# First stage of an attention and expert block on one core: order of projections, masks and small vector work changed

## What is computed

```python
def bi_wkv(r, k, v, w, u, time_emb):          # condition; r = x, k = v = side input
    tf = sigmoid(sum(time_emb, -1))            # one number per batch
    decay = exp(-exp(w)) * (0.5 + 0.5 * tf)    # per channel and batch
    ek, ekv = exp(min(k, 30)), exp(min(k, 30)) * v
    nf, df = forward scans of a * decay + (ekv, ek);  nb, db = the same backward
    euk = exp(min(u + k, 30))
    base = sigmoid(r) * (nf + nb - ekv + euk * v) / max(df + db - ek + euk, 1e-8)
    return base * (0.8 + 0.2 * tf)

def attn(h, Wq, Wk, Wv, Wg, Wd, Wo):           # 16 heads of 128, 4 key heads
    q, k, v = h @ Wq, h @ Wk, h @ Wv
    bias = sigmoid(q @ Wg) * (v @ Wd)          # per key position and key head
    logits = q k / sqrt(128) + bias, causal, and only where bias > 0
    return softmax(logits) v @ Wo

x = x + attn(bi_wkv(x, side, side, w, u, cond), ...)
x = x + experts(bi_wkv(x, side, side, w2, u2, cond), ...)   # 64 experts, top 8
```

## Time and profile before

| | us |
|---|---|
| three timed runs | 525.01, 524.29, 521.43 (median 524.29) |
| the profiled execution | 525.55 |
| its span, first to last instruction | 523.8 |
| mean granted TensorE clock, share of full speed | 0.957 |

### The profile page before, as it was taken

One profiled execution on the slowest core, in us unless ns is written; L12 is line 12 of the kernel. 1 busy time (PEld: TensorE's weight loads), 2 busy tenths in 40 slices (PEclk: granted clock), 3 DMA queues, 4 the chain that ended last, 5 costly groups with the idle time before them and its releaser, 6 DMA issues.

```text
span 523.8 us, 10365 instructions
## 1 busy us (share of the span) xinstructions
PE 454.5 (87%) x3069; PEld 343.3 (66%) x3069; DVE 346.8 (66%) x1206; ACT 308.9 (59%) x852; POOL 213.3 (41%) x224
## 2 busy tenths in 40 slices
PE   3487889999999889998998957869999999999474
PEld 1266677787787668786886653446777777877221
DVE  4948769559658678739859973825567777774044
ACT  4366677689586787968798670113436656665200
POOL 0323402005012265110357877403666666666700
PEclk9879899999999999999999977979999999999969
DMA  7931494100030012300029998499845555560297
GB/s 258 416 147 42 84 193 111 22 1 1 0 81 2 25 69 72 72 11 2 21 76 378 405 405 295 119 304 309 287 138 154 164 156 158 159 166 12 52 404 299
DMA packets 47318, 79.49 MB, mean 152 GB/s; under 512 B 8266, under 2 KB 31127, under 8 KB 46880
## 3 DMA queue, kind: packets, MB, share of 16 engines
q1 hardware_dynamic: 36544, 55.08, 33.7%
q0 software_dynamic: 7680, 16.93, 8.9%
q10 hardware_dynamic: 3040, 6.82, 3.9%
HBM read 56.54 MB, written 26.44 MB: 158 GB/s over the span
## 4 chain that ended last, share of the span: by engine, by line
PE 51%; DVE 16%; ACT 14%; DMA 8%; issue 5%; POOL 3%; SPq 2%; DVEq 0%; POOLq 0%; ACTq 0%
PE ps L1701 11%; PE ps L1403 8%; PE ps L1722 7%; PE ps L1528 6%; ACT lg L696 4%; DVE lg L1039 3%; ACT lg L639 3%; DMA pairs<-pair_rows 3%; PE ps L1451 2%; PE ps L1399 2%; PE ps L1401 2%; PE ps L1400 2%; POOL slot_rows L618 2%; DMA xrow<-slot_rows 2%; SPq L432 2%
## 5 line engine op out<-in xcount | busy, mean ns | idle before, releaser
L625 POOL DMA_INDIRECT pair_rows<-eout,dest x93 | 92.0, 989 | 61.6 <-ACT eout L639 39.7
L696 ACT ACTIVATE lg<-lg,mneg 128x128 f32<-128x128 f32 (+1 forms) x128 | 56.4, 442 | 26.1 <-DVE mneg L1039 26.0
L1701 PE MATMUL ps<-wts,xg 128*64 (+1 forms) x512 | 70.6, 341 | 1.1 <-DVE xg L1316 1.1
L546 POOL DMA_INDIRECT slot_rows<-rows,pair_slot x48 | 48.8, 1017 | 34.7 <-issue 23.6
L1701 PEld LDWEIGHTS ps<-wts,xg 128*64 128x64 f32 x512 | 52.5, 142 | 13.3 <-issue 5.5
L1528 PE MATMUL ps<-oT,wo_sb 128*128 128x256 f32 x240 | 54.4, 380 | 0.0
L1316 DVE COPY xg<-ps 128x512 f32<-128x512 f32 (+1 forms) x50 | 33.3, 666 | 29.7 <-PE ps L1403 26.1
L1528 PEld LDWEIGHTS ps<-oT,wo_sb 128*128 128x128 f32 x240 | 44.6, 190 | 6.2 <-ACT oT L639 0.7
L838 ACT ACTIVATE sact<-ps 128x192 f32<-128x192 f32 (+1 forms) x50 | 16.2, 324 | 52.0 <-PE ps L1701 50.0
L1722 PE MATMUL ps<-wts,aT 96*64 96x256 f32 (+1 forms) x256 | 46.0, 379 | 0.4 <-ACT aT L639 0.4
L639 ACT ACTIVATE lg<-lg,rinv 128x128 f32<-128x128 f32 (+1 forms) x128 | 45.9, 448 | 0.8 <-DVE rinv L1047 0.8
(11 more groups left out here) (237 smaller groups left out, 1189.6 us busy)
## 6 DMA issues: line engine op xcount, KB each, us to landing
wts<-in_experts_dram SPq DMA_DIRECT2D x22, 640.0 KB, 13.9
xrow<-slot_rows SPq DMA_DIRECT2D x188, 65.0 KB
pairs<-pair_rows SPq DMA_DIRECT2D x16, 512.0 KB, 9.5
wts<-in_experts_dram ACTq DMA_DIRECT2D x10, 640.0 KB, 7.0
slot_rows<-zero SPq DMA_DIRECT2D x1, 4160.0 KB, 24.0
wT<-in_wq_t_dram SPq DMA_DIRECT2D x4, 512.0 KB, 6.9
wq_raw<-in_wq_l_dram SPq DMA_DIRECT2D x1, 2048.0 KB, 14.4
wo_sb<-in_wo_l_dram SPq DMA_DIRECT2D x1, 2048.0 KB, 20.2
```

The lines of the kernel that those rows point to most:

```text
L546: nc.gpsimd.indirect_dma_start(out=slot_d, out_offset=bass.IndirectOffsetOnAxis(ap=pair_slot[:, t, k:k + 1], axis=0), in_=r[:, k, :], in_o ...
L625: nc.gpsimd.indirect_dma_start(out=pair_d, out_offset=bass.IndirectOffsetOnAxis(ap=dest[:, d:d + 1], axis=0), in_=out_rows(d), in_offset=N ...
L696: ins = nc.scalar.activation(t, t, ACT.Exp, bias=mneg[:, u % 2, c:c + 1], scale=-1.0, accum_out=rsum[:, u % 2, c:c + 1])
L1701: ins = nc.tensor.matmul(ps[h * R:(h + 1) * R, 2 + u % 2, k * I2:(k + 1) * I2], xg[u % len(xg)][:, k, cc, h * R:(h + 1) * R], moving, star ...
```

## The change

SP issues `cond_b` first instead of third. The condition's sigmoid becomes 1/(1+exp(-s)): DVE negates and caps the sum, ACT takes an exponential after the two for the decay, DVE adds one and takes the reciprocal. ACT loads the exponential's table again with a one-column instruction ahead of `hh`. The first quarter of `wql` moves from POOL to DVE, behind the gate's low part; POOL's second quarter waits for the low part of K(0,1) instead of the bias, and `masks(0)` stands ahead of the products for batch 1. The projections' order becomes G, K(0,0), B, K(0,1), Q(0,0), Q(0,1), V0, scores of round 0, Q(1,0), Q(1,1), V1, scores of round 1. The pieces of batch 1's condition are placed anew on DVE, and `join_scans` now stands behind the logits of round 1.

```diff
-        first_projs = [G, K(0,0), K(0,1), B, Q(0,0), Q(0,1), V0, V1, Q(1,0), Q(1,1)]
+        first_projs = [G, K(0,0), B, K(0,1), Q(0,0), Q(0,1), V0, Q(1,0), Q(1,1), V1]
+        AHEAD_OF_SCORES = 7                       # was 8, on PE
 SP
+            sp.dma_start(cond_b[:], ...)          # first
             sp.dma_start(by_batch(vT, 0), side_t[:, 0])
             sp.dma_start(wu[:], wu_t)
-            sp.dma_start(cond_b[:], ...)
 POOL
-            wq_low(0)
-            pool.wait_ge(bias_ready, 1)
+            pool.wait_ge(proj_lo, order[("K", 0, 1)] + 1)
             wq_low(1)
+            masks(0)
             cond_products((0, 1))
-            masks(0)
             wq_low(2)
 ACT
-            act.wait_ge(tf_sum, 1)
-            nc.scalar.activation(tf[:], tfsum[:], ACT.Sigmoid).then_inc(tf_ready, 1)
             act.wait_ge(ld_wu, 16)
             link(nc.scalar.activation(edec[:], wcols, ACT.Exp))
             nc.scalar.activation(edec[:], edec[:], ACT.Exp, scale=-1.0).then_inc(dec_ready, 1)
+            act.wait_ge(tf_sum, 1)
+            nc.scalar.activation(tf[:], tfsum[:], ACT.Exp).then_inc(tf_ready, 1)
...
+            nc.scalar.activation(scrap[:, 0:1], edec[:, 0, 0:1], ACT.Exp)
+            h_hi_part(0)
             wq_high(0)
-            h_hi_part(0)
-            G, wq_high(1), K(0,0), wq_high(2), K(0,1), B, wq_high(3), cond_exps((0, 1)), Q(0,0), Q(0,1), V0, V1
+            G, wq_high(1), K(0,0), B, cond_exps((0, 1)), K(0,1), Q(0,0), wq_high(2), Q(0,1), wq_high(3), V0
             softmax_exp(0)
             Q(1,0), Q(1,1)
             normalise(0)
+            V1
 DVE
+            V.tensor_scalar(tfsum[:], tfsum[:], -1.0, SIG_CAP, ALU.mult, ALU.min).then_inc(tf_sum, 1)
...
+            link(V.tensor_scalar(tf[:], tf[:], 1.0, None, ALU.add))
+            link(V.reciprocal(tf[:], tf[:]))
...
-            G, K(0,0), K(0,1), B, cond_part(0,1,0), Q(0,0), Q(0,1), cond_part(0,1,1), V0, V1
-            make_logits(0); scan_back(0,1,0); Q(1,0), Q(1,1); row_sums(0)
-            join_scans(0, 1, scan_back(0,1,1)); make_logits(1)
+            G
+            V.tensor_tensor(wql[:, :, w], wq_raw[:, :, w], f32(wqh[:, :, w]), ALU.subtract).then_inc(wq_lo, 1)
+            cond_part(0,1,0); K(0,0), B; ekv; scan_on(0,1,0); K(0,1), Q(0,0), Q(0,1)
+            scan_on(0,1,1); scan_back(0,1,0); V0; make_logits(0); row_sums(0); Q(1,0), Q(1,1)
+            scan_back(0,1,1); make_logits(1); join_scans(0,1); V1
             cond_part(0, 1, 3)
             cond_part(0, 1, 4)
```

More of the change, by code:

```diff
@@ L384, in _ @@
             by_batch = lambda a, b: a[:, :, b * T:(b + 1) * T]
+            sp.dma_start(cond_b[:], cond.rearrange("(o b) d -> o (b d)", o=1).to_broadcast([P, NB * TD])).then_inc(ld_cond, 16)
             sp.dma_start(by_batch(vT, 0), side_t[:, 0]).then_inc(ld_side[0], 16)
             sp.dma_start(wu[:], wu_t).then_inc(ld_wu, 16)
[L387 removed]
             sp.dma_start(wgd_sb[:], wgd_l).then_inc(ld_wgd, 16)
@@ L945, in cond_part @@
                     for cc in range(CC):
-                        dd = d(cc).to_broadcast([P, T])
-                        V.tensor_tensor_scan(out=nf[:, cc, :], data0=dd, data1=ekv[:, cc, :], initial=0.0, op0=ALU.mult, op1=ALU.add)
-                        ins = V.tensor_tensor_scan(out=df[:, cc, :], data0=dd, data1=ek[:, cc, :], initial=0.0, op0=ALU.mult, op1=ALU.add)
+                        ins = scan_on(c, b, cc)
                     link(ins)
@@ L965, in cond_part, with scan_on @@
                         link(V.scalar_tensor_tensor(out=sig[:, :, b * T:(b + 1) * T], in0=nf[:], scalar=ofac[:, b:b + 1], in1=df[:], op0=ALU.mult, op1=ALU.mult))
+            def scan_on(c, b, cc):
+                dd = decay[:, c, cc, b:b + 1].to_broadcast([P, T])
+                V.tensor_tensor_scan(out=nf[:, cc, :], data0=dd, data1=ekv[:, cc, :], initial=0.0, op0=ALU.mult, op1=ALU.add)
+                return V.tensor_tensor_scan(out=df[:, cc, :], data0=dd, data1=ek[:, cc, :], initial=0.0, op0=ALU.mult, op1=ALU.add)
             def rev(a):
@@ L975, in join_scans @@
             def join_scans(c, b, scanned):
-                link(scanned)
+                if scanned is not None:
+                    link(scanned)
                 for cc in range(CC):
@@ L1109, in _ @@
             dve.wait_ge(ld_cond, 16)
-            V.tensor_reduce(tfsum[:], cond_b[:].rearrange("p (b d) -> p b d", b=NB), AX.X, ALU.add).then_inc(tf_sum, 1)
+            link(V.tensor_reduce(tfsum[:], cond_b[:].rearrange("p (b d) -> p b d", b=NB), AX.X, ALU.add))
+            V.tensor_scalar(tfsum[:], tfsum[:], -1.0, SIG_CAP, ALU.mult, ALU.min).then_inc(tf_sum, 1)
             dve.wait_ge(ld_wu, 16)
@@ L1134, in _ @@
             h_lo_part(0)
-            for j in first_projs[:4]:
-                proj_lo_part(j)
+            proj_lo_part(("G", 0, 0))
+            dve.wait_ge(wq_hi, 1)
+            w = slice(0, G * HD)
+            V.tensor_tensor(wql[:, :, w], wq_raw[:, :, w], f32(wqh[:, :, w]), ALU.subtract).then_inc(wq_lo, 1)
             cond_part(0, 1, 0)
-            for j in first_projs[4:6]:
-                proj_lo_part(j)
-            cond_part(0, 1, 1)
-            for j in first_projs[6:8]:
-                proj_lo_part(j)
+            proj_lo_part(("K", 0, 0))
+            proj_lo_part(("B", 0, 0))
+            dve.wait_ge(cond_exp, 2)
+            link(V.tensor_tensor(ekv[:], ek[:], vT[:, :, T:2 * T], ALU.mult))
+            scan_on(0, 1, 0)
+            proj_lo_part(("K", 0, 1))
+            proj_lo_part(("Q", 0, 0))
+            proj_lo_part(("Q", 0, 1))
+            scan_on(0, 1, 1)
+            scan_back(0, 1, 0)
+            proj_lo_part(("V", 0, 0))
             make_logits(0)
-            scan_back(0, 1, 0)
-            for j in first_projs[8:]:
-                proj_lo_part(j)
             row_sums(0)
-            join_scans(0, 1, scan_back(0, 1, 1))
+            proj_lo_part(("Q", 1, 0))
+            proj_lo_part(("Q", 1, 1))
+            ins = scan_back(0, 1, 1)
+            link(ins)
             make_logits(1)
+            join_scans(0, 1, None)
+            proj_lo_part(("V", 0, 1))
             cond_part(0, 1, 3)
@@ L1588, in turn_block @@
                 ins.then_inc(h2_turned, 1)
-            for j in first_projs[:8]:
+            for j in first_projs[:AHEAD_OF_SCORES]:
                 proj(j)
             make_scores(0)
-            for j in first_projs[8:]:
+            for j in first_projs[AHEAD_OF_SCORES:]:
                 proj(j)
```

28 lines of the change are left out of this document (16 added, 12 removed).

## The result

The kernel became slower, by about 1%. Six executions of it have a median of 530.09 us (524.43 to 532.04), six of the kernel before 523.27 (521.43 to 525.01): a ratio of 1.0124 [1.0093, 1.0154]. On a second occasion ten executions had a median of 529.75, nineteen of the kernel before 523.85: 1.0083 [1.0042, 1.0124]. Ratios leave out executions that stand over 1.5% above the fastest of their kernel, which in experiment 4 takes out three of eleven. The profiled execution took 530.06, with a span of 527.9 and a mean granted clock of 0.949 (before 525.55, 523.8 and 0.957).

A forecast was written before the change was run, and what follows sets the result against it. No engine bounds the first stage, a relay of handovers. Gains of 5.8 at round 0's output projection and 5.9 at round 1's normalising were taken as 5.7: 525.55 to 519.85, 518.6 on the median's scale; range 516.8 to 522.3.

The forecast's parts named there:

- The head: Start up to `ekv`: no table load between, side input ends the wait; `ekv` from 9.79 to 7.6, a gain of 2.2.
- The stall goes with `wq_low(0)`: At `hf`, L963 takes 2.71 beside POOL's `wql`, 0.69 elsewhere; moving that quarter off POOL was to gain 2.0.
- Restart at 21.1 plus 6.1 is 27.2: PE's clock returns 6.1 after restart, so K(0,1), starting at 28.1, runs at full clock and ends at 29.8, was 32.97.
- the edit hides behind K(0,0): DVE's `wql` quarter and batch 1's `ek`, `euk` end at 27.4, K(0,0)'s copies at 27.5: 0.1 to spare.
- The masks, to end at 37.5: Before the first logits: bias row at 27.6, masks done at 37.5; logits begin then, a gain of 6.2.
- only the scans between 34.1 and 36.6 meet the masks by my times: DVE's four scans ahead of the first logits, 0.68 each, end at 36.6; argument against POOL holding them longer.
- the clock comes back late: Rival, chance 0.30: clock returns at 31.5, K(0,1) costs 1.6 more; gain 4.6 or 3.0, giving 519.7 to 521.3.
- POOL holds DVE: Rival, chance 0.05, slower: at 31 to 41 us POOL's reading instructions, 7.6, hold DVE's scans; loss of 1.9, 526.2.
- V1 in 1.85 behind Q(1,0): V1 on PE, now behind the scores of round 0, runs 43.1 to 45.0; logits of round 1 end at 48.0.
- The join behind the logits of round 1: `join_scans` (1.6) and POOL's sum (1.3) follow those logits; maximum starts at 51.0, `hf` of batch 1 56.6, gain 4.1 left.
- V 1.85, scores(2) 2.4: PE after `hf` of batch 1: G 1.0, V, scores, then output projection at 62.4 against 68.17, a gain of 5.8.
- What the relay gains reaches the end: No load is under way at 31 to 33, so the first rounds' gain, taken as 5.7, should reach the program's end.

The follow-up runs named there:

- experiment 4: Changed kernel with V1 back ahead of the scores of round 0 on PE, ACT and DVE: 524.01, ratio 0.9979, in two groups.
- experiment 8: Kernel before with only `cond_b` first and the sigmoid from exponentials: 521.48, ratio 0.9960.
- early clock: Executions of the unchanged changed kernel at 524.43 to 525.41 (6 of 18); in the traced 524.89 one the clock rises before 27.
- late clock: Executions of the unchanged changed kernel at 528.39 to 533.55 (12 of 18); in the traced 530.06 one the clock rises near 34.
- 6: Changed kernel with two spare matmuls, whose result nobody reads, behind B on PE: 525.76, ratio 1.0046.
- experiment 7: Changed kernel with POOL's product and third `wql` held back until the logits of round 0 are done: 525.83, ratio 1.0057.
- 9: Kernel before with the new head, `wql`'s first quarter on DVE and the early table load, old orders otherwise: 522.39, ratio 0.9967.
- experiment 3: Changed kernel with `join_scans` ahead of round 1's logits and four scans behind round 0's: 521.48, ratio 0.9957; again 522.94, 0.9999.
- 1: Changed kernel with `join_scans` back ahead of the logits of round 1: 525.79, ratio 1.0038.
- 2: Changed kernel with four scans moved behind the logits of round 0: 524.25, ratio 1.0023.
- 10: Changed kernel with early join, late scans, plus V1 ahead of scores: 522.03; plus two spare matmuls behind B instead: 522.13. Separately, only B behind both keys: 527.65.
- number 3 with spare matmuls: Changed kernel with early join, four scans late and two spare matmuls behind B: 522.13, ratio 0.9972.

## Why the prediction was wrong, point by point

The forecast was 518.6, faster; it measured 530.09, outside the range, on the side that held 0.05.

- **The head** (`ekv` at 7.6, `hf` done at 21.0): right in size. `ekv` starts at 6.94 and `hf` is done at 20.37 in the first trace; over the four traces of the new kernel they stand between 6.90 and 8.50 and between 20.33 and 21.92. The cause named was not: it is `wu`, which "comes along with the side input" in the forecast, that ends the wait for `ek` in all four, at 4.66 to 6.26. Alone the head is worth 1.5 us by the medians (experiment 8), for the 2.2 counted for it. At the first logits its trace stands 2.3 to 2.6 ahead of the two further traces of the kernel before; why less is left of it in the medians is not shown.
- **The stall on `hf`** (2.0 gone): the step "The stall goes with `wq_low(0)`" rested on one execution, and this term failed. The stall hangs on 0.2 us in who comes first; in two more traces of the kernel before, it isn't there (`hf` done at 22.80 and 22.45, was 25.25). The first logits come there at 41.26 and 41.03, not 43.73. So 2.5 us of the 6.2 forecast at that point were not to be had in two of three executions.
- **K(0,1) at full clock from 28.1, "Restart at 21.1 plus 6.1 is 27.2"**: the step failed in two of four traces, and by the times in most executions. The clock did not fall as PE started: G ran at the high level in all four (1.03 to 1.06), and the clock fell at 22.9 to 23.8. It rose at 26.2 and 26.7 in two, and at 33.5 and 34.0 in the others, against 31.5 as my worse end. The delay of 6.1 from one trace was taken for a constant. K(0,1)'s start was right, 28.1 to 28.5 in all four, but in the two late ones by luck: K(0,0) ended at 25.0 and 25.3 and not at 26.5, its copies at 26.06 in the first and not at 27.5, and its low part began only at 27.71. So "the edit hides behind K(0,0)" failed there. The table load, meant for 19.7 to 21.0, ran from 20.87 to 22.15, and ACT copied the gate at 23.74 only, though G was done at 21.97; the gate's low part, DVE's `wql` and `ek`, `euk` for batch 1 held K(0,0)'s low part by 1.65 us, and PE stood for 2.13 ahead of K(0,1).
- **The masks, to end at 37.5**: right, 37.27 to 37.83 in the four traces.
- **The four scans in 2.5 us, "only the scans between 34.1 and 36.6 meet the masks by my times"**: this is the step that decided the sign. It was nearly right for the early clock (scans from 34.66, 3.45 in sum, logits at 38.11 against 37.5), and false for the late one. K(0,1)'s low part releases POOL's second `wql` and Q(0,1), and all that follows on DVE stands behind it. When it is 2.0 late, POOL takes that up: in the early execution its masks wait for the bias row until 35.45, so its product and third `wql` begin at nearly the same time in both. DVE has no such slack. The scans start 2.41 later and run into the product and the third `wql`, which adds 2.71: 6.16 in sum, logits at 43.24. I gave "the clock comes back late" 0.30 and 3.0 us at most, and "POOL holds DVE" 0.05 from 5.7 us of holding on, as two rivals with separate causes. They are one: the late clock brings the meeting about. Experiments 6 and 7 break the link at either end, at the clock or at POOL, and with 525.76 and 525.83 both come to within a microsecond and a half of the early executions.
- **V1 in 1.85 behind Q(1,0)**: failed in the new kernel's executions of both kinds: 3.6 to 3.8. PE waits 3.0 to 3.3 us there for the exponentials and Q(1,0)'s low part, and over 43 to 47 us the granted clock is 0.60 in the early execution. The wait was in my times, and I priced the projection at full clock all the same. There the scores start 3.5 behind V1's start, for 1.9 forecast: 1.6 of the 2.8 by which the end of the logits of round 1 misses the forecast (50.77 for 48.0); 0.6 came from ahead of it, and 0.5 from the scores and logits behind it.
- **The join behind the logits of round 1, `hf` of batch 1 at 56.6**: the direction was right (9.4 from logits to `hf` measured, 8.6 forecast, 5.55 before), a size was off: POOL's next sum holds the maximum, 1.49 for 0.72. The step behind it failed: "V 1.85, scores(2) 2.4". Before, PE came to G of batch 1 without an idle, at 63.24, 2.5 behind `hf`. Now PE is done before `hf`, waits 2.79, and takes 3.76 for V. With the early clock the output projection starts at 68.89 for 62.4 forecast: 0.6 late from the first logits, 2.2 from V1 and the scores behind it, 0.8 from the maximum, 2.9 from G, V and scores of batch 1. With the late clock `hf` of batch 1 is 6.0 later still (66.19 for 60.15, 5.1 of it from the first logits), and G, V and scores, of which more ran at the high level, take 1.6 less: 73.29.
- **What the relay gains reaches the end**: right within some microseconds. From the output projection to the end of the execution it takes 456.8 in the new kernel's trace, 457.4 before, 458.7 with the head alone.

What is shown: the reordering is what costs, not the head (8, 9); the scans' place ahead of the logits and the join's place behind them carry it, since with both taken back it is gone (3). Against the new kernel's 1.0124 each alone takes back 0.9% and 1.0% (1, 2), both together 1.7%, so they nearly add; the repairs 4 and 6 bring nothing on top of them (10). That these two are the only way out is not shown: with V1 alone taken back, seven of eleven executions are at the level of the kernel before (4). **What stays open**: why the clock rises near 26.5 in some executions and near 34 in others of one program. In all four traces of the new kernel it falls between 22.9 and 23.8. In the two early ones `wu` lands later (`ek` starts at 6.26 and 5.92, for 4.70 and 4.66), so `hf` comes later, and PE begins G at 21.7 and 22.1, so K(0,0) runs at the low level, PE is busy up to 26, and the clock rises then. In the two late ones PE begins G at 20.9 and 20.7, K(0,0) is done sooner (at 25.0 and 25.3), and PE stands nearly idle to 28. It would mean that an earlier `hf` delays K(0,1). But in experiment 7 K(0,0) ran at the low level to 26.07 and K(0,1) was slow all the same (3.66), and in experiments 1 and 4 too; so this is no full account, and no run here separates it from chance.

## What to carry to other kernels

A stall of 2 us between two engines that start within 0.2 us of each other can be gone in the next execution, as here in two of three: look at a second execution before it is booked as a gain. When an order is moved, list the DVE instructions with two SBUF inputs (and those with one that a trace shows held, as the maximum here) and the GpSimd instructions within a few microseconds of them on either side, and ask which event, such as a slower projection, would move one of the two and not the other. A projection moved behind a wait of PE (3.0 to 3.3 us ahead of V1 here) is to be priced at the low clock until a trace says otherwise.

## What the runs showed of the hardware

- DVE scans of 0.68 took 0.99, 1.70 and 2.81 beside GpSimd's masks (1.23), product (1.67) and `wql` (2.77), each ending 0.54 to 0.56 behind its neighbour. The hold runs both ways: GpSimd's product took 1.27 undisturbed (experiment 3) and 1.67 beside the scans, and the masks took 1.23 or 1.87.
- A DVE instruction with a single input, the maximum over 128x512, is held as well: 0.42 (number 3 with spare matmuls), 0.72, 1.49 and 2.75 in the runs, by what POOL did beside it.
- One and the same program shows the rise of TensorE's clock behind K(0,0) at 26.2 and 26.7 or at 33.5 and 34.0 us. The Trainium skill (TensorE: Matmul & The Clock Gate, Part 1: The HAM clock gate) says that the number of slow matmuls varies from run to run, which agrees. It also puts the penalty of the ramp under 1% of a typical kernel. Here the two kinds differ by 5.17 of 525 us, 1.0%, of which K(0,1) itself is only 1.79 (3.78 less 1.99); most of the rest is the 2.71 by which POOL holds the scans longer.
